# A block of attention and experts in one kernel: the shared network's weights prepared one stage earlier, and its down product issued two chunks behind

## The chip, the core and the metric

The kernel is one program on one core of a Trainium2 chip. The metric is device time in microseconds (us) of one execution, as the median of several runs. The engines are named as the profile names them: PE is TensorE, DVE is VectorE, ACT is ScalarE, POOL is GpSimd, SP is SyncE, which here only issues DMAs.

## What the reference computes

An input of 4 sequences of 2048 rows of 256 features goes through a modulated attention block and then through a modulated feed-forward block: eight routed experts, of which each row takes the two best, and one shared network that every row goes through. What matters here is the end of it:

```python
def _swiglu_mlp(x, wg, wu, wd):
    return jax.nn.silu(x @ wg) * (x @ wu) @ wd
...
y = jnp.einsum('te,etd->td', combine, expert_out).astype(x.dtype)
return y + _swiglu_mlp(identity, sw_gate, sw_up, sw_down)
...
x = x + gb * _L0_ffn_ref(h, ...)
```

The shared network has 704 hidden features (`sw_gate` and `sw_up` are 256 x 704, `sw_down` is 704 x 256). The modulated rows `h` are 8192 x 256.

## The kernel before, in words

The program runs stage after stage, with a barrier of all engines between two stages: setup, q/k/v, attention, a middle stage (projection, norm, routing), `expert_stage` and, last, `shared_stage`. Every stage has one instruction stream for each engine; the order within a stream is the order of the code, an engine does one thing after another, and semaphores order the engines among each other. Nothing is reordered.

All products of the last two stages run in two parts: a float32 value is split into a "high" part (a copy in float32r) and a "low" part (the value less its high part), and each product is the sum of high x high, low x high and high x low. ACT makes the high part of weights and rows, DVE or POOL the low part by a subtraction.

`expert_stage` goes over 39 blocks of 512 gathered rows. For a block it loads one expert's weights and the rows, splits them, and writes the outcome to DRAM (`made_dram`). In it POOL makes the low parts of two of the three weights.

`shared_stage` goes over 16 units `u` of 512 rows, in two buffers (`slot`). The 704 hidden features are `NC` = 6 chunks: five of 128 and, last, one of 64. In each unit:

- PE: `up(u, i)` (L2184 and on) makes gate and up products of chunk `i` into `ps_g` and `ps_u`, 12 matmuls of 512 columns (for the last chunk 6). It waits until the activation and the product two chunks back are done. `down(u, i)` (L2195 and on) multiplies the hidden chunk with `wd`, 12 matmuls of 256 columns, and waits for `hid_done` of that chunk. PE does `up(i)` and then `down(i - 1)`; after the first `up` of a unit comes the last `down` of the unit before.
- ACT: silu of each chunk (`act_g`, L2086; L2088 for the half chunk). Behind the third one (`i == 2`) it waits for the next unit's loads and makes `h_high` (`high_rows`, L2077).
- DVE: `hidden(u, i)` is three instructions: `hid_f` (L2129), the cast `hid_high` (L2133), the subtraction `hid_low` (L2135). Behind chunk 0 it does `finish` of the unit before, `total` (L2147) and `gated` (L2150); behind chunk 2 `h_low` of the next unit (`low_rows`, L2140); behind chunk 3 `mix_experts`, four `first` (L2114) and four `mix` (L2120), which weigh the rows of the two experts.
- POOL: eight gathers of expert rows for the next unit (`got`, L2051), and then `y_out` of this one (L2064), which waits for `gated`.
- SP: `load(u + 1)` (`h`, L2017, and `x`, L2019, 512 KB each), then the store of `y_out` of unit `u` (L2028). A load waits until the buffer is free: `h2_done` says that its rows have been split, and `out_done` that `y_out` of the unit two back, which reads the same `x` buffer, is made:

```python
            def load(u, slot):
                sp.wait_ge(h2_done, u + 1)
                sp.wait_ge(out_done, u + 1)
```

`out_done` starts at 2 and each `y_out` adds 1; `load(u + 1)` thus waits for `y_out(u - 1)`, and this for `finish(u - 1)`.

Before its first unit the stage loads its weights (L2008 to L2012), ACT copies them (L2096), DVE subtracts (L2174), and PE begins when all is split.

## Time and profile before

| | |
|---|---|
| time, median of 3 runs (lowest, highest) | 3312.66 us (3307.47, 3314.26) |
| the profiled execution: its own time, and its span | 3308.82 us, 3307.1 us |
| PE busy over the span | 2912.5 us, 88% |
| mean granted TensorE clock | 0.944 of full speed |
| last stage, from the barrier (2835.0) to the end of the span | 472.1 us |
| of that, PE's first matmul | 2853.12 |

A row of the timeline reads: start in us, duration in us, engine, line of the kernel, operation, output<-input, shapes, how many instructions are merged in the row, and in brackets how long the engine stood idle before it and on whom it waited. A matmul's duration is the time through the array; its pace is the distance between two starts. The profiled execution's own time is 1.7 us above its span.

### The profile page before, as it was taken

The numbers are of one execution on the slowest core, as the hardware profiler recorded it, in microseconds if no ns is written. First come the engines' busy times: TensorE is split into PE (matmuls) and PEld (weight loads), VectorE is DVE, ScalarE is ACT, GpSimd is POOL, SyncE is SP. The second block draws the span as 40 slices with busy tenths as digits, with TensorE's granted clock in tenths as the row PEclk, the third lists the DMA queues.
The fourth block names the chain that finished last, engine by engine and source line by source line (L and its number), as shares of the span: only waits on it lengthen the run. The fifth ranks groups of instructions, "written<-read, shape, count | busy, mean of one in ns | idle before, by whom it ended". The sixth has DMA issues, their size and how long they took to land. (4 is left out here: it accounts for less than half of the span.)

```text
span 3307.1 us, 61435 instructions
## 1 busy us (share of the span) xinstructions
PE 2912.5 (88%) x22508; PEld 1616.0 (49%) x22508; DVE 2518.0 (76%) x4678; ACT 1588.5 (48%) x2160; POOL 884.5 (27%) x1100
## 2 busy tenths in 40 slices
PE   6885699999999999999999996873999999788888
PEld 3553133333333333333333325763888888677776
DVE  5885989888898888898888914664777777566665
ACT  2542166666676666666666782221444444111111
POOL 5773010111110111101111112664222222333332
PEclk8997699999999999999999997775999999899999
DMA  4776111122111212111221005664444455332332
GB/s 132 204 209 186 49 35 47 48 54 53 43 44 49 54 48 57 38 46 48 55 52 43 20 8 160 212 198 167 155 155 155 156 159 156 105 94 85 96 97 73
DMA packets 388533, 317.93 MB, mean 96 GB/s; under 512 B 112720, under 2 KB 374844, under 8 KB 388288
## 3 DMA queue, kind: packets, MB, share of 16 engines
q1 hardware_dynamic: 370752, 277.67, 29.4%
q0 software_dynamic: 12288, 33.57, 3.0%
q10 hardware_dynamic: 5248, 3.41, 0.4%
q8 instruction: 155, 2.54, 0.3%
q14 instruction: 90, 0.74, 0.1%
HBM read 196.89 MB, written 116.93 MB: 95 GB/s over the span
## 5 line engine op out<-in xcount | busy, mean ns | idle before, releaser
L903 ACT ACTIVATE probs<-ps_s 128x1024 f32<-128x1024 f32 (+3 forms) x1280 | 1077.9, 896 | 599.2 <-PE ps_s L1071 598.6
L926 DVE TENSOR_REDUCE piece_rest<-ps_m 128x1 f32<-128x512 f32 (+2 forms) x1260 | 748.8, 646 | 91.8 <-PE ps_m L1046 42.0
L1071 PE MATMUL ps_s<-q_st,k_st 50*128 50x512 bf16 (+7 forms) x5120 | 594.4, 346 | 19.0 <-ACT probs L903 15.2
L1086 PE MATMUL ps_o<-probs,vs 128*32 128x512 f32 (+3 forms) x5120 | 600.8, 541 | 4.3 <-POOL probs L883 1.2
L883 POOL TENSOR_SCALAR_AFFINE_SELECT probs<-probs 128x256 f32<-128x256 f32 x512 | 204.9, 406 | 1481.2 <-ACT probs L903 1476.0
L926 DVE TENSOR_REDUCE piece_late<-ps_m 128x1 f32<-128x512 f32 x900 | 548.8, 666 | 33.0 <-PE ps_m L1038 17.9
L1038 PE MATMUL ps_m<-k_st,q_st 48*128 48x512 bf16 (+3 forms) x2400 | 407.5, 353 | 65.8 <-DVE piece_rest L926 48.1
L1038 PEld LDWEIGHTS ps_m<-k_st,q_st 48*128 48x128 bf16 x2400 | 106.9, 93 | 651.8 <-DVE piece_rest L926 339.0
L1071 PEld LDWEIGHTS ps_s<-q_st,k_st 50*128 50x128 bf16 (+1 forms) x5120 | 224.1, 95 | 250.8 <-ACT probs L903 91.0
L1803 ACT ACTIVATE act_g<-ps_g 128x512 f32<-128x512 f32 x117 | 69.9, 597 | 279.5 <-PE ps_u L1895 279.5
L1840 DVE TENSOR_TENSOR hid_f<-act_g,ps_u 128x512 f32<-128x512 f32 x117 | 80.5, 688 | 126.8 <-ACT act_g L1803 126.8
L1086 PEld LDWEIGHTS ps_o<-probs,vs 128*32 128x32 f32 x5120 | 101.2, 108 | 142.8 <-issue 96.9
L2086 ACT ACTIVATE act_g<-ps_g 128x512 f32<-128x512 f32 x80 | 47.5, 595 | 251.1 <-PE ps_u L2191 206.3
L1765 POOL TENSOR_TENSOR wu_low<-wu,wu_high 128x768 fp32r<-128x768 f32 x39 | 76.8, 1968 | 326.1 <-ACT wu_high L1791 326.1
L2202 PE MATMUL ps_d<-sd_high,hid_high 128*128 128x256 f32 x384 | 114.0, 297 | 47.5 <-DVE hid_low L2135 46.2
L1359 POOL DMA_INDIRECT expert_rows<-rows,at x128 | 133.3, 1041 | 66.9 <-issue 36.0
L1845 DVE TENSOR_TENSOR hid_low<-hid_f,hid_high 128x512 fp32r<-128x512 f32 x117 | 138.8, 1187 | 4.0
L2051 POOL DMA_INDIRECT got<-expert_made,at_now x128 | 128.7, 1006 | 49.1 <-issue 36.8
L1907 PE MATMUL ps_d<-wd_high,hid_high 128*128 128x256 f32 x468 | 136.0, 291 | 1.2 <-DVE hid_low L1845 1.2
L1907 PE MATMUL ps_d<-wd_low,hid_high 128*128 128x256 f32 x468 | 132.1, 282 | 0.0
L1907 PE MATMUL ps_d<-wd_high,hid_low 128*128 128x256 f32 x468 | 132.0, 282 | 0.0
L621 PE MATMUL ps_qk<-wqkv,h_t 128*128 128x512 f32 x256 | 122.8, 603 | 1.0 <-ACT h_t L559 1.0
(228 smaller groups left out, 5103.2 us busy)
## 6 DMA issues: line engine op xcount, KB each, us to landing
k_st<-qk_parts SPq DMA_DIRECT2D x768, 32.0 KB, 1.8
qk_parts<-parts SPq DMA_DIRECT2D x124, 192.0 KB, 2.9
q_st<-qk_parts SPq DMA_DIRECT2D x720, 32.0 KB, 1.8
x_r<-expert_rows SPq DMA_DIRECT2D x39, 512.0 KB, 4.6
expert_made<-made SPq DMA_DIRECT2D x39, 512.0 KB, 2.9
x_in<-in_L_attn_x_dram SPq DMA_DIRECT2D x32, 512.0 KB, 4.7
vs<-v_ones SPq DMA_DIRECT2D x64, 256.0 KB, 3.7
v_ones<-v_out SPq DMA_DIRECT2D x60, 256.0 KB, 4.7
```

The lines of the kernel that those rows point to most:

```text
L621: pe.matmul(ps_qk[:, t % 2, :], h_t[:, slot, c, t * P:(t + 1) * P], wqkv[:, c, 0:QK], start=(c == 0), stop=(c == DC - 1))
L883: pool.affine_select(out=block_now, in_=block_now, compare_op=ALU.is_ge, fill=0.0, base=0, pattern=[[0, 2], [1, P]], channel_multiplier=-1 ...
L903: act.activation(probs[:, u % PSLOTS, 2 * pair:2 * pair + 2, j * P:ST], ps_s[:, pair, :, j * P:ST], ACT.Exp, scale=SCALE).then_inc(exp_don ...
L926: v.tensor_reduce(dst, ps_m[:, bank, 0:n * w].rearrange("p (n w) -> p n w", n=n), AX.X, ALU.max) \
L1038: last[z] = pe.matmul(bank[:, i * w:(i + 1) * w], q_st[rows, slot, 0, a + i, qi * P:(qi + 1) * P], k_st[rows, slot, 0, a + i, kt * ST:kt * ...
L1071: last = pe.matmul(ps_s[:, pair, z, j * P:ST], k_st[rows, slot, half, pair, kc * P:(kc + 1) * P], q_st[rows, slot, half, pair, qt * ST + j ...
L1086: last = pe.matmul(ps_o[h * VW:(h + 1) * VW, j * P:ST], vs[:, slot, kc, h * VW:(h + 1) * VW], probs[:, u % PSLOTS, h, j * P:ST], start=(kc ...
L1359: pool.indirect_dma_start(rows_dram, bass.IndirectOffsetOnAxis(at[:, rslot, j:j + 1], 0), rows[:, rslot, j % TPS, :], None).then_inc(scatt ...
L1845: v.tensor_tensor(hid[1][:, i, :], hid_f[:, half, :], hid[0][:, i, :], ALU.subtract).then_inc(hid_done, 1)
L1907: last = pe.matmul(ps_d[:, t, :], hid[a][:, i, t * P:(t + 1) * P], wd_p[b][:, slot, i, :], start=(i == 0 and t % 2 == 0 and k == 0), stop= ...
L2051: pool.indirect_dma_start(got[:, slot, j, :], None, made_dram, bass.IndirectOffsetOnAxis(at_now[:, slot, j:j + 1], 0)) \
L2202: last = pe.matmul(ps_d[:, slot, t, :], hid[a][:, i % GS, t * P:(t + 1) * P], wd_p[b][:, i, :], start=(i == 0 and t % 2 == 0 and k == 0), ...
```

## The change

It has three parts.

1. The stage's weights and first rows are loaded in `expert_stage`. The buffers are now made ahead of both stages. SP issues six DMAs (five for weights, one for the rows of unit 0) behind the loads of the first two blocks. Behind its last block ACT makes the four high parts, DVE two low parts of the weights ahead of `take_made` and `h_low` of unit 0 behind it, and POOL the low part of `wd`. `shared_stage` begins with everything split.
2. `down` runs `LAG` = 2 chunks behind `up`: PE does `up(i)` and then `down(i - 2)`; the first two `up` of a unit are followed by the last two `down` of the unit before.
3. DVE's `finish` of the unit before and the copies of `weight_now` and `gb_now` stand behind chunk 2 instead of chunk 0, and `low_rows` behind chunk 4 instead of chunk 2. `mix_experts` stays behind chunk 3, and ACT's `high_rows` behind its third silu.

```diff
@@ expert_stage, SP, behind the first two blocks' loads
+            sp.wait_ge(padded, 4)
+            wg_s, wu_s, wd_s = W["wg"], W["wu"], W["wd"]
...
+            sp.dma_start(wg_s[:, :, 0:FS], sw_gate.rearrange("(c p) f -> p c f", p=P)).then_inc(next_in, 16)
+            sp.dma_start(wg_s[:, :, FS:SNC * P], up_cols[:, :, SFULL * P:FS]).then_inc(next_in, 16)
+            sp.dma_start(wu_s[:, :, :], up_cols[:, :, 0:SFULL * P]).then_inc(next_in, 16)
+            sp.dma_start(wd_s[:, 0:SFULL, :], sw_down[0:SFULL * P, :].rearrange("(j p) n -> p j n", p=P)).then_inc(next_in, 16)
+            sp.dma_start(wd_s[P - SHALF:P, SFULL, :], sw_down[SFULL * P:FS, :]).then_inc(next_in, 16)
+            sp.dma_start(W["h2"][:, 0, :, :].rearrange("p c t -> p (c t)"), h2_dram[0:P, :]).then_inc(next_in, 16)
@@ expert_stage, POOL, behind its last block
+            pool.wait_ge(next_high, 4)
+            pool.tensor_tensor(W["wd_p"][1][:, :, :], W["wd"][:, :, :], W["wd_p"][0][:, :, :], ALU.subtract)
@@ expert_stage, ACT, behind its last block
+            act.wait_ge(next_in, 16 * NEXT_DMAS)
+            for src, dst in ((W["wg"], W["wg_p"]), (W["wu"], W["wu_p"])):
+                act.activation(dst[0][:, :, :], src[:, :, :], ACT.Copy).then_inc(next_high, 1)
+            act.activation(W["h2_p"][0][:, 0, :, :], W["h2"][:, 0, :, :], ACT.Copy).then_inc(next_high, 1)
+            act.activation(W["wd_p"][0][:, :, :], W["wd"][:, :, :], ACT.Copy).then_inc(next_high, 1)
@@ expert_stage, DVE, behind its last block
+            for k, (src, dst) in enumerate(((W["wg"], W["wg_p"]), (W["wu"], W["wu_p"]))):
+                v.wait_ge(next_high, k + 1)
+                v.tensor_tensor(dst[1][:, :, :], src[:, :, :], dst[0][:, :, :], ALU.subtract)
             take_made(NB - 1, 0, NB // 2)
+            v.wait_ge(next_high, 3)
+            v.tensor_tensor(W["h2_p"][1][:, 0, :, :], W["h2"][:, 0, :, :], W["h2_p"][0][:, 0, :, :], ALU.subtract)
@@ shared_stage, ACT ahead of its first unit
-            act.wait_ge(w_in, 16 * W_DMAS)
-            act.wait_ge(padded, 1)
-            for src, dst in ((wg, wg_p), (wu, wu_p), (wd, wd_p)):
-                act.activation(dst[0][:, :, :], src[:, :, :], ACT.Copy).then_inc(w_high, 1)
-            high_rows(0, 0, 1)
+            act.sem_inc(h2_high, 1)
@@ shared_stage, DVE
                         hidden(u, i)
-                        if i == 0 and not (first and slot == 0):
+                        if i == LAG and not (first and slot == 0):
                             finish(u - 1, 1 - slot)
-                        if i == 0 and slot == 0:
+                        if i == LAG and slot == 0:
...
-                        if i == 2 and not (last and slot):
+                        if i == LAG + 2 and not (last and slot):
                             low_rows(u + 1, 1 - slot)
@@ shared_stage, PE
                         up(u, i, slot)
-                        if i > 0:
-                            down(u, i - 1, slot)
+                        if i >= LAG:
+                            down(u, i - LAG, slot)
                         elif not (first and slot == 0):
-                            down(u - 1, NC - 1, 1 - slot)
+                            down(u - 1, NC + i - LAG, 1 - slot)
```

The first place is DVE in the last unit but one, from its first chunk. Names: `act_g` is the silu, `hid_f`, `hid_high` and `hid_low` the hidden chunk and its parts, `total` and `gated` are `finish` of the unit before, `h_low` is `low_rows` of the unit behind. Before:

```order
L2129 TENSOR_TENSOR hid_f<-act_g,ps_u 128x512 [waits p5_hid,p5_silu]
L2133 CAST hid_high<-hid_f 128x512 [waits p5_down,p5_product]
L2135 TENSOR_TENSOR hid_low<-hid_f,hid_high 128x512 [waits p5_hid_high]
L2147 TENSOR_TENSOR total<-ps_d,mix 128x1024 [waits p5_gated,p5_got_used,p5_down]
L2150 TENSOR_TENSOR gated<-total,gb_now 128x1024 [waits p5_out,p5_summed]
L2163 COPY weight_now<-weight_all 128x16 [waits p5_got_used,p5_gated]
L2164 COPY gb_now<-gb 128x256
L2129 TENSOR_TENSOR hid_f<-act_g,ps_u 128x512 [waits p5_hid,p5_silu,p5_now]
L2133 CAST hid_high<-hid_f 128x512 [waits p5_down,p5_product]
L2135 TENSOR_TENSOR hid_low<-hid_f,hid_high 128x512 [waits p5_hid_high]
```

The same unit in the changed kernel, from its third chunk:

```order
L2150 TENSOR_TENSOR hid_f<-act_g,ps_u 128x512 [waits p5_hid,p5_silu]
L2154 CAST hid_high<-hid_f 128x512 [waits p5_down,p5_product]
L2156 TENSOR_TENSOR hid_low<-hid_f,hid_high 128x512 [waits p5_hid_high]
L2168 TENSOR_TENSOR total<-ps_d,mix 128x1024 [waits p5_gated,p5_got_used,p5_down]
L2171 TENSOR_TENSOR gated<-total,gb_now 128x1024 [waits p5_out,p5_summed]
L2184 COPY weight_now<-weight_all 128x16 [waits p5_got_used,p5_gated]
L2185 COPY gb_now<-gb 128x256
L2150 TENSOR_TENSOR hid_f<-act_g,ps_u 128x512 [waits p5_hid,p5_silu,p5_now]
L2154 CAST hid_high<-hid_f 128x512 [waits p5_down,p5_product]
L2156 TENSOR_TENSOR hid_low<-hid_f,hid_high 128x512 [waits p5_hid_high]
L2135 TENSOR_SCALAR first<-got,weight_now 128x256 [waits p5_gathered0]
```

`finish` has moved behind the third `hid_low`; the silu that the next `hid_f` waits for stands on ACT behind `high_rows`, in both kernels, and `h_low` has gone from ahead of `first` to behind the chunk after `mix`.

The second place is DVE at the end of `expert_stage`. Before, behind the last block's last cast:

```order
L1845 TENSOR_TENSOR hid_low<-hid_f,hid_high 128x512 [waits p4_hid_high]
L1850 COPY made<-ps_d 128x1024 [waits p4_stored0,p4_down]
L1656 UNCONDITIONAL_BRANCH
L2102 UNCONDITIONAL_BRANCH [waits barrier_Pool_Activation_PE_DVE_SP_release]
L2174 TENSOR_TENSOR sg_low<-sg_w,sg_high 128x1536 [waits p5_w_high]
L2174 TENSOR_TENSOR su_low<-su_w,su_high 128x1280 [waits p5_w_high]
L2174 TENSOR_TENSOR sd_low<-sd_w,sd_high 128x1536 [waits p5_w_high]
L2140 TENSOR_TENSOR h_low<-h_5,h_high 128x1024 [waits p5_h2_high]
```

And now:

```order
L1881 TENSOR_TENSOR hid_low<-hid_f,hid_high 128x512 [waits p4_hid_high]
L1907 TENSOR_TENSOR sg_low<-sg_w,sg_high 128x1536 [waits p4_next_high]
L1907 TENSOR_TENSOR su_low<-su_w,su_high 128x1280 [waits p4_next_high]
L1886 COPY made<-ps_d 128x1024 [waits p4_stored0,p4_down]
L1910 TENSOR_TENSOR h_low<-h_5,h_high 128x1024 [waits p4_next_high]
L1671 UNCONDITIONAL_BRANCH
L2123 UNCONDITIONAL_BRANCH [waits barrier_Pool_Activation_PE_DVE_SP_release]
L2150 TENSOR_TENSOR hid_f<-act_g,ps_u 128x512 [waits p5_hid,p5_silu]
```

Two subtractions stand ahead of the copy of the last block's outcome, one behind it, and the one of `wd` is POOL's.

## Rows read from the trace of the kernel before

**Rows 1.** The page's first part: busy time, share, instructions.
```profile
PE 2912.5 (88%) x22508; PEld 1616.0 (49%) x22508; DVE 2518.0 (76%) x4678; ACT 1588.5 (48%) x2160; POOL 884.5 (27%) x1100
```
**Rows 2.** Waits from 2866 to 3283: total us, times, longest.
```profile
ACT h_high L2077 <- DMA x<-x_mid: 81.8, 14, 7.2
...
PE ps_d L2202 <- DVE hid_low L2135: 45.0, 40, 3.2
```
**Rows 3.** Timeline of one unit, engines and the DMA queue, 3074 to 3101.
```profile
3074.72 0.40 PE L2191 MATMUL ps_g<-h_high,sg_high 128*128 128x512 f32 x1
...
3077.67 0.60 ACT L2086 ACTIVATE act_g<-ps_g 128x512 f32<-128x512 f32 x1 [5.42 <-PE ps_u L2191]
...
3080.09 1.22 DVE L2147 TENSOR_TENSOR total<-ps_d,mix 128x1024 f32<-128x1024 f32 x1
...
3081.34 1.22 DVE L2150 TENSOR_TENSOR gated<-total,gb_now 128x1024 f32<-128x1024 f32 x1
...
3082.71 2.52 POOL L2064 TENSOR_TENSOR y_out<-gated,x 128x1024 f32<-128x1024 f32 x1 [13.95 <-issue]
...
3085.26 0.38 SPq L2028 DMA_DIRECT2D out_dram<-y_out  x1
...
3085.99 0.60 ACT L2086 ACTIVATE act_g<-ps_g 128x512 f32<-128x512 f32 x1 [3.56 <-PE ps_u L2191]
...
3086.24 0.93 SPq L2019 DMA_DIRECT2D x<-x_mid  x1
...
3091.88 1.06 ACT L2077 ACTIVATE h_high<-h 128x1024 fp32r<-128x1024 f32 x1 [5.29 <-DMA x<-x_mid]
...
3092.84 0.58 ACT L2086 ACTIVATE act_g<-ps_g 128x512 f32<-128x512 f32 x1
...
3092.97 1.22 DVE L2140 TENSOR_TENSOR h_low<-h,h_high 128x1024 fp32r<-128x1024 f32 x1 [4.48 <-issue]
...
3095.97 1.20 DVE L2114 TENSOR_SCALAR first<-got,weight_now 128x256 f32<-128x256 f32 x4
...
3096.10 0.38 PE L2202 MATMUL ps_d<-sd_high,hid_high 128*128 128x256 f32 x1 [1.25 <-DVE hid_low L2135]
...
3098.79 0.68 DVE L2129 TENSOR_TENSOR hid_f<-act_g,ps_u 128x512 f32<-128x512 f32 x1
...
3099.96 0.69 DVE L2135 TENSOR_TENSOR hid_low<-hid_f,hid_high 128x512 fp32r<-128x512 f32 x1
```
**Rows 4.** Timeline of ACT: third silu of units 0, 1 and 15.
```profile
2865.39 0.60 ACT L2086 ACTIVATE act_g<-ps_g 128x512 f32<-128x512 f32 x1 [3.74 <-PE ps_u L2191]
...
2889.43 0.60 ACT L2086 ACTIVATE act_g<-ps_g 128x512 f32<-128x512 f32 x1 [3.56 <-PE ps_u L2191]
...
3282.91 0.60 ACT L2086 ACTIVATE act_g<-ps_g 128x512 f32<-128x512 f32 x1 [3.56 <-PE ps_u L2191]
```
**Rows 5.** Timeline of PE: where it resumes with its clock down.
```profile
2853.12 0.76 PE L2191 MATMUL ps_g<-h_high,sg_high 128*128 128x512 f32 x1 [22.73 <-DVE h_low L2140]
...
2858.10 0.40 PE L2191 MATMUL ps_g<-h_high,sg_high 128*128 128x512 f32 x1
...
3264.54 0.58 PE L2202 MATMUL ps_d<-sd_high,hid_high 128*128 128x256 f32 x1 [2.93 <-DVE hid_low L2135]
```
**Rows 6.** Timeline of several engines around the seam, 2814 to 2850.
```profile
2814.91 1.97 POOL L1769 TENSOR_TENSOR wd_low<-wd,wd_high 128x768 fp32r<-128x768 f32 x1 [1.40 <-ACT wd_high L1794]
...
2815.21 2.21 DVE L1845 TENSOR_TENSOR hid_low<-hid_f,hid_high 128x512 fp32r<-128x512 f32 x1
...
2826.13 0.60 ACT L1803 ACTIVATE act_g<-ps_g 128x512 f32<-128x512 f32 x1 [3.58 <-PE ps_u L1895]
...
2830.42 1.23 DVE L1850 COPY made<-ps_d 128x1024 f32<-128x1024 f32 x1 [1.79 <-PE ps_d L1907]
...
2835.00 0.39 SPq L2008 DMA_DIRECT2D sg_w<-in_L_ffn_sw_gate_dram  x1
...
2845.54 1.48 ACT L2096 ACTIVATE sg_high<-sg_w 128x1536 fp32r<-128x1536 f32 x1 [18.81 <-DMA sd_w<-in_L_ffn_sw_down_dram]
```

More of the change, by code:

```diff
@@ L54 @@
 E, F, FS = 8, 352, 704
+SNC = -(-FS // P)
+SFULL = FS // P
+SHALF = FS - SFULL * P
 EPS = 1e-5
@@ L156, in block_kernel, with late @@
                      steps_dram, plan_dram)
-        expert_stage(nc, C, rows_dram, made_dram, w_gate, w_up, w_down)
-        shared_stage(nc, C, h2_dram, x1_dram, made_dram, sw_gate, sw_up, sw_down, out_flat)
+        with ExitStack() as last:
+            def late(name, shape, dt=F32):
+                return last.enter_context(nc.sbuf_tensor(name, shape, dt))
+            W = dict(
+                wg=late("sg_w", [P, DC, SNC * P]), wu=late("su_w", [P, DC, SFULL * P]), wd=late("sd_w", [P, SNC, D]),
+                wg_p=[late(f"sg_{part}", [P, DC, SNC * P], F32R) for part in PARTS],
+                wu_p=[late(f"su_{part}", [P, DC, SFULL * P], F32R) for part in PARTS],
+                wd_p=[late(f"sd_{part}", [P, SNC, D], F32R) for part in PARTS],
+                h2=late("h2_5", [P, 2, DC, ST]),
+                h2_p=[late(f"h2_{part}", [P, 2, DC, ST], F32R) for part in PARTS],
+            )
+            expert_stage(nc, C, W, rows_dram, made_dram, w_gate, w_up, w_down, h2_dram, sw_gate, sw_up, sw_down)
+            shared_stage(nc, C, W, h2_dram, x1_dram, made_dram, out_flat)
 def stand_alone(eng, held):
@@ L1691, in expert_stage @@
         padded = sem("p4_padded")
+        next_in = sem("p4_next_in")
+        next_high = sem("p4_next_high")
+        NEXT_DMAS = 6
         w_high = sem("p4_w_high")
@@ L1758, in _ @@
             pool.wait_ge(padded, 3)
+            pool.memset(W["wd"][0:P - SHALF, SFULL, :], 0.0).then_inc(padded, 1)
+            pool.wait_ge(padded, 4)
             pool.sem_inc(wu_done, 1)
@@ L1940, in shared_stage @@
     GS = 3
+    LAG = 2
     PICKS = TOPK * TPS
@@ L1952, in shared_stage @@
         gb, weight, made_at = C["gb"], C["weight"], C["made_at"]
-        wg = sb("sg_w", [P, DC, NC * P])
-        wu = sb("su_w", [P, DC, full * P])
-        wd = sb("sd_w", [P, NC, D])
-        wg_p = [sb(f"sg_{part}", [P, DC, NC * P], F32R) for part in PARTS]
-        wu_p = [sb(f"su_{part}", [P, DC, full * P], F32R) for part in PARTS]
-        wd_p = [sb(f"sd_{part}", [P, NC, D], F32R) for part in PARTS]
-        h2_p = [sb(f"h2_{part}", [P, 2, DC, ST], F32R) for part in PARTS]
-        h2 = sb("h2_5", [P, 2, DC, ST])
+        wg_p, wu_p, wd_p, h2, h2_p = (W[k] for k in ("wg_p", "wu_p", "wd_p", "h2", "h2_p"))
         x1 = sb("x1_5", [P, 2, TPS, D])
@@ L2007, in _ @@
         def _(sp):
-            sp.dma_start(wg[:, :, 0:FS], sw_gate.rearrange("(c p) f -> p c f", p=P)).then_inc(w_in, 16)
-            sp.dma_start(wg[:, :, FS:NC * P], sw_up.rearrange("(c p) f -> p c f", p=P)[:, :, full * P:FS]).then_inc(w_in, 16)
-            sp.dma_start(wu[:, :, :], sw_up.rearrange("(c p) f -> p c f", p=P)[:, :, 0:full * P]).then_inc(w_in, 16)
-            sp.dma_start(wd[:, 0:full, :], sw_down[0:full * P, :].rearrange("(j p) n -> p j n", p=P)).then_inc(w_in, 16)
-            sp.dma_start(wd[UPPER, full, :], sw_down[full * P:FS, :]).then_inc(w_in, 16)
             def load(u, slot):
@@ L2016, in load @@
                 sp.wait_ge(out_done, u + 1)
-                sp.dma_start(h2[:, slot, :, :].rearrange("p c t -> p (c t)"), h2_dram[ds(u * P, P), :]) \
-                    .then_inc(in_done[slot], 16)
+                if u:
+                    sp.dma_start(h2[:, slot, :, :].rearrange("p c t -> p (c t)"), h2_dram[ds(u * P, P), :]) \
+                        .then_inc(in_done[slot], 16)
+                else:
+                    sp.sem_inc(in_done[slot], 16)
                 sp.dma_start(x1[:, slot, :, :], x1_dram[ds(u * ST, ST), :].rearrange("(t p) d -> p t d", p=P)) \
@@ L2038, in _ @@
         def _(pool):
-            pool.memset(wd[0:P - HALF_CHUNK, full, :], 0.0).then_inc(padded, 1)
-            pool.wait_ge(padded, 1)
             pool.sem_inc(out_done, 2)
@@ L2170, in body @@
                             mix_experts(u, slot, it)
-            for k, (src, dst) in enumerate(((wg, wg_p), (wu, wu_p), (wd, wd_p))):
-                v.wait_ge(w_high, k + 1)
-                v.tensor_tensor(dst[1][:, :, :], src[:, :, :], dst[0][:, :, :], ALU.subtract).then_inc(w_done, 1)
-            low_rows(0, 0)
             body(0, True, False)
@@ L2221, in _ @@
                 body(it, False)
-            down(NST - 1, NC - 1, 1)
+            for i in range(NC - LAG, NC):
+                down(NST - 1, i, 1)
 _INS = ['L0_attn_x', 'L0_attn_w_qkv', 'L0_attn_w_proj', 'L0_attn_b_proj', 'L0_ffn_gate_w', 'L0_ffn_w_gate',
```

13 lines of the change are left out of this document (4 added, 9 removed).

## The prediction, made before the changed kernel ran

> **What bounds the kernel now.** I read the page's first part, the waits of the last stage, and then one unit of it as a timeline; the other stages keep their instructions, apart from six DMA issues and a memset. PE is busy for 88% of the span [rows 1], but in the last stage two kinds of wait stand out [rows 2]: PE waits 45.0 us, 40 times, for `hid_low` ahead of `down`, and ACT waits 81.8 us, 14 times, for the next unit's loads ahead of `h_high`. The first is what a `down` two chunks behind takes away. The second is the one to look at. ACT takes things in order, so its fourth silu stands behind `h_high`, and `h_high` behind a load that is issued only after `y_out` of the unit before. The reader should see this as one chain in the timeline [rows 3]: first silu 3077.67, `total` 3080.09, `gated`, `y_out` 3082.71, store issue 3085.26, load issue 3086.24, `h_high` 3091.88, fourth silu 3092.84. It takes 15.17 us. It starts at the unit's first silu, while PE goes on in chunks of 4.16 us (3085.99 less 3077.67, halved); by its end PE has waited only 1.25 us (3096.10). A unit lasts (3282.91 - 2889.43) / 14 = 28.11 us from third silu to third silu [rows 4].
>
> **The unit after the change.** `finish` now stands behind `hidden(2)`, two chunks later. The load still waits for `y_out` of the unit before, and ACT's `high_rows` still stands ahead of the fourth silu. So the same 15.17 us now start at the third silu, where the fourth is due 4.16 us later. I go round the loop once from the third silu, all from [rows 3]:
>
> - third silu to `total` 2.42, to `y_out` 2.62, to the store's issue 2.55, to `h_high` 6.62, to the fourth silu 0.96: together 15.17.
> - Late loads: over 14 units ACT's wait for them has a mean of 81.8 / 14 = 5.84 us [rows 2] against 5.29 in this unit: +0.55. They had some cover before, now none.
> - fourth silu to the end of `hidden(3)` 2.42 (as the first silu to `total`), `first` and `mix` 2.82 (3095.97 to 3098.79), `hidden(4)` 1.86 (3098.79 to 3100.65).
> - `h_low` of the next unit 1.22; it now stands here, and PE waits for it ahead of the next unit's `up(0)`.
> - PE from `up(0)` to the third silu: 3085.99 - 3074.72 = 11.27. This part holds three `up` and two `down`, as before.
>
> The sum is 35.3 us, against 28.11. Is PE really out of work? Behind the third silu it has `down(0)`, `up(3)`, `down(1)`, `up(4)`, `down(2)`, which end 9.5 us after it: 2 x 4.16 and a `down` of 1.4, less 0.2. (`up(0)` takes 2.95 us from its start at 3074.72 to the silu; with 0.2 of that for the hand-over, a choice of mine, an `up` is 2.75 and a `down` the other 1.4 of 4.16.) `up(5)` needs the fourth silu and its product, at 15.7 + 1.3 = 17.0: a wait of 7.5 us (1.3 is the silu's 0.6 and `hid_f`'s 0.7). Behind it stand `down(3)` and the next unit, until `h_low` at 24.0. DVE idles in the same hole, since `hidden(3)` needs that silu; POOL's gathers run there and are needed only a unit later. The loop is taken by the loads of units 2 to 15, 14 times: 14 x (35.3 - 28.11) = +100.7 us. The 40 short waits for `hid_low` are gone, but they lie inside the 28.11 that the new period replaces, so nothing more is gained for them.
>
> **The clock.** After a stall of 2.93 us PE resumed at half pace (its `down` at 3264.54 is a matmul of 0.58 us where 0.38 is usual), while the wait of 1.25 left it at full pace [rows 3, 5]. The longest of the 40 waits is 3.2 us [rows 2], so such a fall is rare before. A hole of 7.5 us will set it to 1.2 GHz in each unit. `up(5)` and `down(3)` at half pace still end at 17.0 + 2 x 2.8 = 22.6, before `h_low`. What counts is whether the clock is back at `up(0)`, 7 us after the resumption, with a second hole of some 2 us between. An `up(0)` at half pace takes 4.98 us (2858.10 - 2853.12) instead of 2.75 [rows 5]: 2.2 more. The bounds are 0 and, if `down` behind it is slow too, 3.6 a unit. I take half an `up`, 1.1, for 14 units: +15. The Trainium skill says in "TensorE: Matmul & The Clock Gate" (HAM oscillation) that where a loop waits for a DMA in every tile, the gate closes in every tile and the penalty is paid each time. The stall of 2.93 us agrees; by that rule each unit pays in full, and that is the first rival below.
>
> **The seam.** Before, PE began the stage at 2853.12 [rows 5], 18.1 us behind the barrier, for loading and splitting [rows 6]. Now ACT copies behind its last silu (2826.73): 1.48 for 1536 columns [rows 6], so by size 5.2 for all four, to 2832.0. POOL's subtraction of 1536 columns is twice its 768 of 1.97: to 2835.9. DVE does two subtractions (by size from `h_low`, 1.8 and 1.5) from 2828.6 (2826.13 and 2.42, as from silu to `total`), then `made`, to 2833.2 where it ended at 2831.65; the barrier came 3.35 us after that end, so 2836.6. `h_low` falls beside POOL: a subtraction of 0.69 [rows 3] took 2.21 beside POOL's [rows 6], so I let it wait until 2835.9, to 2837.1. With half a microsecond for the barrier PE begins at 2837.6: -15.5. If the copy `made` were held by POOL too, the barrier would come 3 us later. The Trainium skill ("SBUF — State Buffer", two separate sides) says that the port pair that both engines share is locked against an operation with two SBUF inputs. `made` reads PSUM and would pass; by that rule the seam stays at 2837.6. The trace shows no `made` beside POOL.
>
> From there to unit 1's third silu it was 36.3 us; now `up(0)` at half pace 4.98, two more `up` without a `down` 5.5, 0.2 to the silu, and a full-pace unit 23.6: 34.3, I take 34.6, so -1.7. The loads of this stretch are issued at once and hide.
>
> **What costs nothing.** The six DMA issues of SP (0.4 to 0.9 us each by [rows 3], so 2 to 6 us) stand behind both blocks' loads and ahead of a store that is due a block later. If the cover were gone, PE's second block would lose up to 6 us; I take 0. The tail: the last `down` no longer waits for its chunk, -0.5.
>
> **Sum.** Span 3307.1 - 15.5 - 1.7 - 0.5 + 100.7 + 15 = 3405; own time 1.7 above it: 3407. The profiled execution before took 3308.82, the median was 3312.66, 3.8 more. Forecast: **3411 us**, 3.0% slower.
>
> **Rivals.**
>
> - *The clock stays low at the start of every unit*, through `up(0)` and the `down` behind it: 3.6 instead of 1.1 a unit, +35: 3446. For it: the second hole, and the rule above. Against: at 2853.12 the clock was back after 5 us of work [rows 5]. 14%.
> - *Faster: the loads land before the fourth silu needs them*, and the lag does what it can. Place: store issue to `h_high`. Then PE never waits and a unit lasts 5 x 4.16 + 2.8 = 23.6: 3411 - 15 - 14 x 11.7 = 3232. It decides where the loop has lost (100.7 + 15 - 17.7) / 14 = 7.0 us: below that price the kernel is faster. From the store's issue to `h_high` it would have to be 0.2 us instead of 7.2 (6.62 and 0.55), so only if the load did not wait for `y_out` at all. The code and the order of issues in [rows 3] (store, then loads, 0.03 us behind `y_out`) speak against it. 4%.
> - *The chain is read rightly but does not bind*: something that I left out, such as a shorter way from `finish` to the load, gives back most of the 7.2 us a unit and leaves about the time of before: 3312. 2%.
> - The forecast with the clock's term between 0 and 2 a unit, and the seam 3 us either way: 3392 to 3430. 80%.
>
> **How the numbers follow.** The forecast and the clock rival hold 94%. The range of the likeliest is 3392 to 3430; I take 3385 to 3440 for 8 in 10, with the lower end for loads that always land as in [rows 3] (-8) and a hole that does no harm. What a measurement of this kernel can tell from no change is about 0.2%, 6.6 us. Faster 5%, the same 2%, slower 93%.
>
> **What would show it.** ACT: the fourth silu of units 1 to 14 starts about 15.7 us after the third, with `h_high` waiting some 12 to 14 us for the load. PE: one wait of 7 to 8 us ahead of the last `up` of a unit, on a silu or its product, and one of 1.5 to 3 ahead of the next unit's first, on `h_low`; no more on `hid_low`. Third silu to third silu 35 to 37 us. Granted clock in the last stage near 0.85. PE's first matmul of the stage at 2837 to 2841. The prediction is wrong if the period is under 30 us, or if the fourth silu doesn't stand behind `h_high`.

## The result: 3.5% slower, and the profile after

| | before | after |
|---|---|---|
| time, median (lowest to highest) | 3312.72 us (3307.47 to 3314.26), 4 runs | 3429.70 us (3422.96 to 3433.95), 4 runs |
| ratio to before, 95% interval | | 1.0354 [1.0334, 1.0374] |
| profiled execution, own time and span | 3308.82, 3307.1 us | 3433.95, 3432.2 us |
| mean granted TensorE clock | 0.944 | 0.927 |
| a unit of the last stage | 28.11 us | 37.46 us |

The forecast was 3411 us, with 3385 to 3440 around it. The first part of the page after has the same number of matmuls as before [rows 1], but 44 us more of PE's busy time, and a smaller share:

```profile
PE 2956.3 (86%) x22508; PEld 1658.9 (48%) x22508; DVE 2494.7 (73%) x4677; ACT 1587.0 (46%) x2160; POOL 878.5 (26%) x1101
```

The waits of the last stage after, from 2866 to the end of the span (engine, instruction, whom it waited for: total us, times, longest single one), which answer to [rows 2]:

```profile
ACT h_high L2102 <- DMA x<-x_mid: 204.6, 14, 15.1
...
PE ps_g L2208 <- DVE hid_f L2150: 88.0, 11, 8.4
...
PE ps_g L2208 <- DVE h_low L2161: 30.2, 15, 2.3
PE ps_g L2208 <- ACT act_g L2111: 23.4, 3, 7.9
...
PE ps_d L2219 <- DVE hid_low L2156: 0.8, 2, 0.5
```

The wait that the distance of two chunks was to take away is gone: 45.0 us before `down`, now 0.8. In its place stand 14 waits of about 8 us (88.0 and 23.4 together), and 15 of 2 us for `h_low`. Above them ACT's wait for the load has grown from 81.8 us to 204.6.

One unit as a timeline, ACT, DVE, POOL, PE and the DMA queue in order of time, answers to [rows 3]:

```profile
3107.53 0.60 ACT L2111 ACTIVATE act_g<-ps_g 128x512 f32<-128x512 f32 x1 [3.56 <-PE ps_u L2208]
...
3109.95 1.22 DVE L2168 TENSOR_TENSOR total<-ps_d,mix 128x1024 f32<-128x1024 f32 x1
...
3112.57 2.39 POOL L2089 TENSOR_TENSOR y_out<-gated,x 128x1024 f32<-128x1024 f32 x1 [24.68 <-issue]
...
3114.99 0.38 SPq L2055 DMA_DIRECT2D out_dram<-y_out  x1
...
3115.48 0.44 SPq L2042 DMA_DIRECT2D h<-h_t  x1
...
3123.00 1.06 ACT L2102 ACTIVATE h_high<-h 128x1024 fp32r<-128x1024 f32 x1 [14.87 <-DMA x<-x_mid]
...
3123.96 1.06 ACT L2111 ACTIVATE act_g<-ps_g 128x512 f32<-128x512 f32 x2
...
3125.41 0.77 PE L2208 MATMUL ps_g<-h_high,sg_high 128*128 128x512 f32 x1 [8.18 <-DVE hid_f L2150]
...
3131.08 1.22 DVE L2161 TENSOR_TENSOR h_low<-h,h_high 128x1024 fp32r<-128x1024 f32 x1
...
3132.36 0.66 PE L2208 MATMUL ps_g<-h_high,sg_high 128*128 128x512 f32 x1 [2.22 <-DVE h_low L2161]
...
3136.99 0.60 ACT L2111 ACTIVATE act_g<-ps_g 128x512 f32<-128x512 f32 x1 [8.06 <-PE ps_u L2208]
...
3145.31 0.60 ACT L2111 ACTIVATE act_g<-ps_g 128x512 f32<-128x512 f32 x1 [3.56 <-PE ps_u L2208]
```

The loop can be read off row by row. The third silu (3107.53) lets `total` go, then `y_out`, the store, the load, and `h_high` 15.47 us later. The fourth and fifth silu, merged in one row, stand right behind it, though the fourth's products had been there for long (`up(3)`'s last matmul started at 3111.27). PE's last `up` waits 8.18 us, DVE works off its queue until `h_low`, and the next unit's first `up` starts at 3132.36. From third silu to third silu that is 37.78 us; over 14 units it is 37.46, from two rows of ACT's timeline that answer to [rows 4]:

```profile
2882.79 0.60 ACT L2111 ACTIVATE act_g<-ps_g 128x512 f32<-128x512 f32 x1 [3.56 <-PE ps_u L2208]
...
3407.27 0.60 ACT L2111 ACTIVATE act_g<-ps_g 128x512 f32<-128x512 f32 x1 [3.56 <-PE ps_u L2208]
```

The seam, where the expert stage ends, answers to [rows 6]. The rows are of ACT, DVE and POOL, and PE's first matmul of the last stage:

```profile
2830.55 0.60 ACT L1834 ACTIVATE act_g<-ps_g 128x512 f32<-128x512 f32 x1 [3.58 <-PE ps_u L1936]
2831.05 1.48 ACT L1849 ACTIVATE sg_high<-sg_w 128x1536 fp32r<-128x1536 f32 x1
...
2834.53 1.47 ACT L1851 ACTIVATE sd_high<-sd_w 128x1536 fp32r<-128x1536 f32 x1
...
2836.05 1.22 DVE L1886 COPY made<-ps_d 128x1024 f32<-128x1024 f32 x1
...
2836.08 3.42 POOL L1806 TENSOR_TENSOR sd_low<-sd_w,sd_high 128x1536 fp32r<-128x1536 f32 x1 [14.78 <-ACT sd_high L1851]
...
2837.18 3.40 DVE L1910 TENSOR_TENSOR h_low<-h,h_high 128x1024 fp32r<-128x1024 f32 x1
...
2841.19 0.77 PE L2208 MATMUL ps_g<-h_high,sg_high 128*128 128x512 f32 x1 [6.37 <-DVEq L2127]
```

From the last silu to PE's first matmul it was 26.99 us [rows 5, 6]; it is now 10.64. That is the gain of the change, 16.35 us. The last silu itself came 4.42 us later in this execution than in the one before: 4.05 of that had gathered in the stages ahead of `expert_stage`, whose work nobody touched, and 0.37, at most the price of the six added DMAs, between the start of `expert_stage` and that silu.

**Where the time went**, by spans: 4.05 (earlier stages) + 0.37 - 16.35 (seam) + 5.29 (unit 0 and the start of unit 1: 41.60 us from PE's first matmul to unit 1's third silu, against 36.31) + 14 x (37.46 - 28.11) = 130.9 + 0.74 (the end) = 125.0; measured 3432.2 - 3307.1 = 125.1.

### The profile page after: what moved, and what is told of

The parts are those of the page before. It is cut to its first block and busy times, and to the rows that moved or that the text cites. A ratio compares the mean times of both kernels' runs of the same rounds, so it can differ in the third digit from the quotient of the medians.

```text
span 3432.2 us, 61434 instructions
## 1 busy us (share of the span) xinstructions
PE 2956.3 (86%) x22508; PEld 1658.9 (48%) x22508; DVE 2494.7 (73%) x4677; ACT 1587.0 (46%) x2160; POOL 878.5 (26%) x1101
## 3 DMA queue, kind: packets, MB, share of 16 engines
q8 instruction: 155, 2.54, 0.3%
## 5 line engine op out<-in xcount | busy, mean ns | idle before, releaser
L1086 PE MATMUL ps_s<-q_st,k_st 50*128 50x512 bf16 (+7 forms) x5120 | 595.2, 346 | 19.0 <-ACT probs L918 15.2
L941 DVE TENSOR_REDUCE piece_late<-ps_m 128x1 f32<-128x512 f32 x900 | 549.1, 667 | 33.9 <-PE ps_m L1053 17.3
L2150 DVE TENSOR_TENSOR hid_f<-act_g,ps_u 128x512 f32<-128x512 f32 x80 | 54.8, 685 | 299.3 <-ACT act_g L2111 160.5
L2208 PE MATMUL ps_g<-h_high,sg_high 128*128 128x512 f32 x192 | 90.8, 473 | 147.9 <-DVE hid_f L2150 88.0
L1876 DVE TENSOR_TENSOR hid_f<-act_g,ps_u 128x512 f32<-128x512 f32 x117 | 80.5, 688 | 127.3 <-ACT act_g L1834 127.3
L2089 POOL TENSOR_TENSOR y_out<-gated,x 128x1024 f32<-128x1024 f32 x16 | 39.1, 2445 | 374.9 <-issue 338.5
```

The costliest lines, as they stand in the source:

```text
L941: v.tensor_reduce(dst, ps_m[:, bank, 0:n * w].rearrange("p (n w) -> p n w", n=n), AX.X, ALU.max) \
L1086: last = pe.matmul(ps_s[:, pair, z, j * P:ST], k_st[rows, slot, half, pair, kc * P:(kc + 1) * P], q_st[rows, slot, half, pair, qt * ST + j ...
L1876: v.tensor_tensor(hid_f[:, half, :], act_g[:, half, :], ps_u[:, half, :], ALU.mult).then_inc(product, 1)
L2208: last = pe.matmul(dst[:, i % 2, :], w[a][:, c, i * P:(i + 1) * P], h2_p[b][:, slot, c, :], start=(k == 0), stop=(k == DC * len(PRODUCTS) ...
```

## Experiments

The theory was the *load chain*: the load of the next unit's rows hangs on `finish`, and ACT's fourth silu on that load. Its rivals: *the distance itself* (a `down` two chunks behind makes the loop long, wherever `finish` stands), and *the work moved into the seam*. Below, `DOWN` is the distance of `down`, `FIN` the chunk behind which `finish` stands, `LOW` that of `low_rows`. The kernel after is 2, 2, 4 and the kernel before 1, 0, 2. Each ratio is to runs of the kernel before on the same chip.

**1. The seam alone.**

```diff
-    LAG = 2
+    DOWN, FIN, LOW = 1, 0, 2
```

> The changed kernel with the order of the last stage put back: down one chunk behind, finish and the copies behind chunk 0, low_rows behind chunk 2. Only the work moved into expert_stage is left of the change. Theory L (the lag moved finish, and with it the load and ACT's fourth silu, two chunks later): the units are those of before, 28.1 us from third silu to third silu, and the seam gives its 16 us: 3313 - 16 - 2 = 3295 us, up to 3301 if the 6 us that unit 0 lost come with the seam. Theory W (the loss comes with the weights' new place, by their addresses or by DMAs in another stage): still above 3400 us.

3300.23 us (3297.59 to 3304.67, 9 runs), ratio 0.9969 [0.9959, 0.9979]. The seam is not what made the kernel slow; it is worth 0.3%. From last silu to first matmul it took 10.63 us, as in the kernel after, so the seam gains 16.4 us here too. But the spans differ by 9.7 only: from PE's first matmul to unit 1's third silu it took 43.33 us against 36.31, and ACT's third and fourth silu of unit 0 are late with no engine named (the profile's word is `remote`). More on this in 9.

```profile
2849.25 0.60 ACT L2111 ACTIVATE act_g<-ps_g 128x512 f32<-128x512 f32 x1 [6.31 <-remote]
...
2858.50 0.60 ACT L2111 ACTIVATE act_g<-ps_g 128x512 f32<-128x512 f32 x1 [7.71 <-remote]
```

**2. The distance alone**, in the kernel before: `down` two chunks behind, with `finish` and `low_rows` where the change has them, and no work moved across the seam.

```diff
-                        if i == 0 and not (first and slot == 0):
+                        if i == LAG and not (first and slot == 0):
                             finish(u - 1, 1 - slot)
```

> The kernel before with the lag alone: down two chunks behind, finish and the copies behind chunk 2, low_rows behind chunk 4; weights loaded and split in the last stage as before. Theory L: a unit lasts 37.5 us as in the changed kernel, and the seam costs its 16 us again: 3430 + 16 = 3446 us, or 3440 without unit 0's 6 us. Theory W: near 3313 us.

3438.65 us (3437.50 to 3444.08, 4 runs), ratio 1.0392 [1.0374, 1.0409]; 37.45 us a unit (from `h_high` of unit 2 to that of unit 15, by 13). The whole loss is this part.

**3. `finish` back to chunk 1, and to chunk 0**, `down` still two behind; one run each.

```diff
-    LAG = 2
+    DOWN, FIN, LOW = 2, 1, 4
```

> The changed kernel with finish and the copies behind chunk 1 instead of chunk 2; the lag of down stays at two chunks. Theory L: y_out, the load, h_high and the fourth silu all come 4.2 us sooner, a unit lasts 33.3 us, 14 x 4.2 = 58 us less: 3371 us. Theory D (two chunks of lag are slow in themselves, by PE waiting for silu or by its clock): no change, 3430 us.

> The same with finish and the copies behind chunk 0, where DVE has to wait for the last down of the unit before, which PE now does behind up(1). Theory L: total starts some 5.7 us after the first silu instead of 10.7 (third silu 8.3 and 2.4), so a unit is 5 us shorter than in the changed kernel, 32.4 us: 3360 us, and less if PE's hole gets too short for the clock to fall. Theory D: 3430 us.

3356.96 us and 3354.34 us (single runs, no interval), 32.55 and 32.08 us a unit. The distance is the same and the loss is more than halved, so most of the loss isn't the distance itself. One chunk earlier gives back 4.9 us a unit, 0.7 more than a chunk of 4.16, and the time was 14 us below what I expected. The trace shows where 0.5 of the 0.7 is: in 5 of 14 units TensorE's clock was up at the next unit's first `up`, and over all 14 that took 4.17 us to its silu on average, where the kernel after needs 4.65 (see 6). The second chunk gives only 0.5. Why so little is a row of the waits of the second kernel:

```profile
DVE total L2168 <- PE ps_d L2219: 49.0, 16, 3.4
```

`finish` at chunk 0 waits there for the last `down` of the unit before, which PE makes only behind `up(1)`: 49.0 us in 16 waits, 3.06 on average. So the distance has a price on this chain after all. The prediction has nothing of it; the expectation of this run had.

**4. The load freed from the chain.** `h` is loaded a unit earlier on a semaphore of its own, as soon as its buffer is free, and ACT waits for `h` alone; `x` still waits for `y_out`. With the distance 2 (`DOWN, FIN, LOW = 2, 2, 2`), and with 1 (`1, 0, 2`).

```diff
+            def load_h(u, slot):
                 sp.wait_ge(h2_done, u + 1)
-                sp.wait_ge(out_done, u + 1)
...
+                    if not last:
+                        load_h(u + 2, slot)
                     if not (last and slot):
-                        load(u + 1, 1 - slot)
+                        load_x(u + 1, 1 - slot)
...
-                act.wait_ge(in_done[slot], turn_no * 32)
+                act.wait_ge(h_in[slot], turn_no * 16)
```

> The changed kernel with the load split: the rows h of unit u + 2 are issued as soon as unit u has split its own (one unit ahead), on their own semaphore, and only x waits for y_out; ACT's high_rows waits for h alone; low_rows is back behind chunk 2, behind finish. down stays two chunks behind. Theory L (what costs is that ACT's fourth silu stands behind a load that waits for y_out): no hole in PE, a unit at PE's own pace of 23.6 to 24.3 us, 14 x (28.1 - 23.9) = 59 us below the kernel before and 16 more for the seam: 3238 us. Theory D (the lag is slow in itself): above 3400 us.

> The same split of the load with down one chunk behind and finish behind chunk 0, as before. Theory L: ACT's wait is gone here too; what stays are short waits of PE for hid_low, above all behind first and mix (0.4 to 1 us a unit): 24.6 us a unit, 3250 us. So the lag, on this ground, is worth some 10 us. If the lag is worth nothing, both are the same; if the waits for hid_low stay at 1.5 us twice a unit, 3275 us.

3254.81 us (3250.09 to 3255.36, 5 runs), ratio 0.9816 [0.9803, 0.9829], and 3254.02 us (3252.99 to 3260.93, 5 runs), ratio 0.9818 [0.9805, 0.9831]; 24.77 and 24.70 us a unit. With the load off the chain the kernel after turns from 3.5% slower to 1.8% faster, and `h_high` waits for no DMA. The first version also puts `low_rows` back behind chunk 2, which was not tried alone; in the kernel after PE's waits for `h_low` add up to 30.2 us and the clock behind them costs 1.7 us a unit, together about 4 of the 12.7 us by which the unit got shorter, so the most of it is the load. The first came 17 us above what I expected, and the distance, with the places of `finish` and `low_rows` that go with it, was worth nothing. Both keep a wait of PE, of the version with distance 2 in the whole last stage and then of that with 1 from 2866 to 3230:

```profile
PE ps_g L2212 <- DVE hid_f L2154: 12.9, 13, 1.4
```

```profile
PE ps_d L2223 <- DVE hid_low L2160: 10.4, 25, 2.3
```

The last number of such a row is the longest single wait: on average they are 1.0 and 0.4 us. The expectations below take it for the length of each.

**5. The next unit's rows split first**: `h_high` behind the first silu, `h_low` at chunk 0 or 1, where DVE has time, so that the later hidden values come sooner.

```diff
-                        if i == 2 and not (last and slot):
+                        if i == 0 and not (last and slot):
                             high_rows(u + 1, 1 - slot, it + (1 + slot))
```

> The version with the early load of h and the down product two chunks behind (e5_early_h, 3254.81 us, period 24.80 us), with the next unit's first rows ahead of the hidden values: h_high behind the first silu and h_low at chunk 0. In e5_early_h the PE waited 13 times 1.4 us for hid_f in the last stage. Load-chain theory: h is there more than a unit ahead, so nothing waits for a DMA; if the rows ahead of the last hidden values are what the PE waits for, the period falls by about 1.1 us to 23.7 us and the time to about 3239 us. Rival (the hidden values of the first chunks are then delayed instead by the h_low now ahead of them, 1.2 us): no change, 3252 to 3258 us.

> The same with the down product one chunk behind (e6_early_h_lag1, 3254.02 us, period 24.70 us, PE waits for hid_low 26 times 2.3 us in it): finish at 0, h_high behind the first silu, h_low at chunk 1. If the second chunk of distance is worth anything once h comes early, this one stays above e7_rows_first, at 3245 to 3250 us, since each wait for hid_low costs the PE what the distance would cover; if the distance is worth nothing, both give the same, about 3240 us.

With distance 2 (`2, 2, 0`) 3231.81 us (3228.90 to 3234.09, 5 runs), ratio 0.9760 [0.9747, 0.9773], 23.60 us a unit. With distance 1 (`1, 0, 1`) 3252.95 us (3247.61 to 3254.87, 5 runs), ratio 0.9821 [0.9808, 0.9835], 24.80 us a unit. Now the second chunk of distance is worth 21 us, again with `finish` and `low_rows` at the places that go with it. From 2866 to 3170 in the first of them PE has no gap (window, its length, then busy us and instructions of PE, weight loads, DVE, ACT and POOL; clock; DMA share; GB/s):

```profile
2866.00:3170.00 304.00, 304.00 (x1782) 269.30 (x1781) 245.09 (x388) 58.40 (x91) 132.33 (x124) 1.00 0.35 109
```

23.60 is what the prediction worked out for a unit that never waits (5 x 4.16 + 2.8). This version is the fastest of all: 79 us below the kernel before on its chip. It came 7 us below what I expected, the other 3 above; part of the 7 may lie in unit 0, where PE had no gap this time (28.00 us busy from 2842 to 2870), though a silu of ACT was late there too.

**6. The loads ahead of the store**, in the kernel after.

```diff
-                    if not (last and slot):
-                        load(u + 1, 1 - slot)
+                    if not u:
+                        load(1, 1)
                     sp.wait_ge(out_done, u + 1 + 2)
+                    if u + 2 < NST:
+                        load(u + 2, slot)
                     sp.dma_start(out_flat[ds(u * ST, ST), :].rearrange("(t p) d -> p t d", p=P), y_out[:, :, :]) \
```

> The changed kernel with the loads of h and x of the unit after next issued on SP ahead of the store of y_out, behind the same wait for y_out. Queue theory: the landing of h, 8.0 us from the store's issue to h_high, holds 0.5 us of issue and some 1.2 to 1.5 us of the store's own 512 KB that go ahead of the load; the loop is then 1.7 to 2.0 us a unit shorter, 14 times, less nothing else: 3402 to 3406 us. If the store's transfer shares the engines with the loads wherever it stands, only the issue is saved, 7 us: about 3423 us. If neither counts, 3430 us.

3393.41 us (3389.81 to 3395.32, 4 runs), ratio 1.0248 [1.0232, 1.0264]; 36 us below the kernel after, more than the queue theory gave. The store ahead of the loads did cost about what it said: over 14 units `h_high` now comes 6.14 us after the first issue on average, not 7.69, and ACT's waits for the load add up to 183.8 us instead of 204.6, 1.5 us less a unit (1.7 to 2.0 were expected). But a unit is 34.70 us, 2.8 less. The rest is the clock. A *hole* here is a stretch in which PE has no work; the kernel after has two in each unit, one ahead of the last `up` and one ahead of the next unit's first. These are matmuls of PE in one unit of this version: the last `up`, the end of the `down` behind it, and the start of the next unit's first `up`.

```profile
3138.29 0.77 PE L2210 MATMUL ps_g<-h_high,sg_high 128*128 128x512 f32 x1 [6.40 <-issue]
3138.85 0.63 PE L2210 MATMUL ps_g<-h_low,sg_high 128*128 128x512 f32 x1
3139.28 0.63 PE L2210 MATMUL ps_g<-h_high,sg_low 128*128 128x512 f32 x1
...
3143.34 0.41 PE L2221 MATMUL ps_d<-sd_high,hid_low 128*128 128x256 f32 x1
3145.07 0.51 PE L2210 MATMUL ps_g<-h_high,sg_high 128*128 128x512 f32 x1 [1.31 <-DVE h_low L2163]
3145.41 0.39 PE L2210 MATMUL ps_g<-h_low,sg_high 128*128 128x512 f32 x1
3145.64 0.40 PE L2210 MATMUL ps_g<-h_high,sg_low 128*128 128x512 f32 x1
```

After 6.40 us without work PE resumes at 1.2 GHz (starts 0.43 us apart). After the second, shorter hole of 1.31 it resumes at 2.4 GHz (0.23 apart) and stays there: `up(0)` to its silu takes 3.05 us. So it was in 12 of 14 units, with second holes of 1.31 to 1.73 us. In two, behind 1.79 and 1.93, the clock fell during `up(0)`, which took 4.61 and 4.64; these units lasted 36.2 and 36.4 us, the others 34.2 to 34.6. In the kernel after, this hole was 1.73 to 2.31 us and `up(0)` took 4.63 to 4.66 in 14 of 14 units. The hole's length is not the only thing that differs: behind the first hole the clock was back after 3.5 to 4.6 us in the kernel after, here in no unit before 4.58 and in 9 of 14 not until the second hole. Where it comes back earlier, `down(3)` ends earlier and the second hole is longer, so these runs don't tell the two apart.

**7. `h_high` behind the fourth silu**, in the kernel after.

```diff
-                        if i == 2 and not (last and slot):
+                        if i == 3 and not (last and slot):
                             high_rows(u + 1, 1 - slot, it + (1 + slot))
```

> The changed kernel with ACT's h_high of the next unit behind the fourth silu (chunk 3) and not ahead of it, everything else as it is. Load-chain theory: the fourth silu, and with it the last hidden values, no longer wait for the load; the loop loses what stands between h_high and the last up products but still waits for h_low and h_high ahead of up(0) of the next unit, so it gets shorter by about 4.9 us a unit, some 69 us: about 3361 us, more if the clock still falls in each unit. Rival D (the down product's distance of two chunks is itself what makes the loop long): 3430 us as before.

3363.29 us (3361.99 to 3367.60, 4 runs), ratio 1.0161 [1.0146, 1.0177]; 32.70 us a unit, 4.8 less than after, where 4.9 was expected. So the order of ACT's two instructions is the other half of the loop. With no distance changed and no load moved, more than half of the loss goes.

**8. PE's holes filled** with matmuls of 128x256 that nobody reads, in the kernel after: 60 ahead of the last `up` of a unit and 30 ahead of the first of the next.

```diff
+                    if u > 1:
+                        fill(slot, 30)
                     pe.wait_ge(h2_done, u + 3)
...
+                        if u and i == NC - 1 and u < NST - 1:
+                            pe.wait_ge(summed, u + 2)
+                            fill(1 - slot, 60)
                         up(u, i, slot)
```

> The changed kernel with matmuls whose result nobody reads, in the PE's own holes: 60 of 128x256 ahead of the last up product of each unit and 30 ahead of the first of the next, at 0.117 us each 7.0 of the 8.2 us and 3.5 of the about 4 us that the PE stands still there. The loop of load, silu and product is untouched. Clock theory: the PE then enters the last up product and the first of the next unit at 2.4 GHz; up(0) to its silu takes 2.95 us again and not 4.63, which is 1.7 us a unit, 14 times, 24 us: about 3406 us. If the clock is not what made up(0) slow, or if it lies beside the loop, 3430 us; if the added matmuls delay the real ones, above 3430 us.

3413.83 us (3410.81 to 3417.05, 4 runs), ratio 1.0310 [1.0293, 1.0327]. PE's stretches in one unit: the filling, the next unit's first matmul, and the silu that it leads to.

```profile
3118.78 3.76 PE L2226 MATMUL ps_d<-sd_high,sg_high 128*128 128x256 f32 x30
3122.72 0.50 PE L2208 MATMUL ps_g<-h_high,sg_high 128*128 128x512 f32 x1 [0.19 <-DVE h_low L2161]
3123.06 0.39 PE L2208 MATMUL ps_g<-h_low,sg_high 128*128 128x512 f32 x1
```

```profile
3125.79 0.60 ACT L2111 ACTIVATE act_g<-ps_g 128x512 f32<-128x512 f32 x1 [7.10 <-PE ps_u L2208]
```

From `up(0)` to its silu it now takes 3.07 us instead of 4.63: the clock was what made it slow, and 1.6 us a unit its price. The kernel gained 16 us, not 24: `h_high` came 15.63 us behind the third silu on average (14.84 to 17.64), not 15.22, so that a unit is 36.27 us, 1.2 less. Why the load took 0.4 longer there, the runs don't show. More work for PE, less time: it would be no remedy, since it treats what the loop leaves behind.

**9. Unit 0.** In the kernel after, its fourth silu is late as well, and no engine is named:

```profile
2853.08 0.60 ACT L2111 ACTIVATE act_g<-ps_g 128x512 f32<-128x512 f32 x1 [3.36 <-PE ps_u L2208]
...
2863.11 0.60 ACT L2111 ACTIVATE act_g<-ps_g 128x512 f32<-128x512 f32 x1 [8.49 <-remote]
```

Of the 8.49 us ACT stood 7.1 with its products there (`up(3)`'s last matmul started at 2855.58 and took 0.39). The trace has three loads and 16 gathers in this stretch, eight for unit 0 and eight for unit 1. The experiment holds the second eight back:

```diff
                 pool.wait_ge(got_used, u + 1)
+                if u == 1:
+                    pool.wait_ge(silu_done, 2 + 5)
```

> The changed kernel with the eight gathers of unit 1 held in POOL's queue until the fifth silu of unit 0; nothing else moves. In the changed kernel's trace the fourth silu of unit 0 came 5.9 us late (2863.11 where the spacing before it, 4.16 us after 2853.08, puts it at 2857.24), with waits that name no engine of this kernel, while 98 us-rate gathers (98 to 115 GB/s) and copies of x ran. If the gathers beside it are the cause, unit 0 loses these 5.9 us and the time is about 3424 us; if the delay belongs to the entry of the stage whatever moves beside it, the fourth or fifth silu of unit 0 is late by 5 to 6 us again and the time is 3430 us (up to 3432 us if unit 1 then waits for the gathers).

```profile
2847.41 0.60 ACT L2113 ACTIVATE act_g<-ps_g 128x512 f32<-128x512 f32 x1 [2.12 <-PE ps_u L2210]
...
2851.57 0.60 ACT L2113 ACTIVATE act_g<-ps_g 128x512 f32<-128x512 f32 x1 [2.61 <-PE ps_u L2210]
```

The fourth silu comes 4.16 us after the third, on time, and from PE's first matmul (2837.38) to unit 1's third silu (2871.26) it takes 33.88 us instead of 41.60. The prediction had 34.6. So the silu is late because those eight gathers run there, right behind the first eight. Gathers alone don't do it: the held ones ran from 2857.75 on, and the silus beside them kept their 4.16 us. From PE's first matmul to the end of the span it took 583.0 us against 591.0, so the gain of 7.7 is kept. In the medians it is small: 3423.23 us (3420.42 to 3425.43, 4 runs), ratio 1.0340 [1.0323, 1.0357], whose interval overlaps that of the kernel after. What ACT waits for there (`remote`) the trace doesn't say.

## Why the prediction was right, and where its sizes were off

- **The chain round the unit: right.** It was read from the trace of before, and each link is there after: third silu to `total` 2.42 (2.42), to `y_out` 2.62 (2.62), to the store's issue 2.42 (2.55), to the fourth silu through `h_high` 8.97 (8.13 with the 0.55 for late loads). Experiments 3, 4 and 7 break it at three places, and each time more than half of the loss goes: 3357 us where the chain gave 3371, 3255 where it gave 3238, 3363 where it gave 3361. Its signs came as listed, most a little above their size: the fourth silu 16.2 us after the third (15.7), a wait of 14.6 for the load (12 to 14), holes of 7.5 to 8.4 and 1.7 to 2.3, a unit of 37.46 (35 to 37), a granted clock of 0.86 from 2883 to 3407 (0.85).
- **The late loads: mis-sized.** I took 14.76 us from third silu to `h_high`; the mean is 15.2 (204.6 / 14 of waiting, and 0.6 of silu): +0.45 a unit. What makes the 0.45 is open. Experiment 6 shows only a part of the whole: with the store's 512 KB ahead of the loads on the same queue `h_high` comes 1.5 us later than without.
- **The clock: right that it falls in each unit, mis-sized.** `up(0)` to its silu took 4.63 us instead of 2.95 [rows 3], 1.68 a unit where I took 1.1. The rival with 3.6 is refuted, for the clock was back before `down` behind it. I had taken the fall ahead of the last `up` and asked whether the clock would still be low at `up(0)`. It was back by then, 3.5 to 4.6 us after PE resumed, and fell a second time, at `up(0)` itself, behind the hole of 2 us. I had sized it from stalls of 1.25 and 2.93 us [rows 3, 5], and this one lay between. I had also read only one row of the four longest waits of the kernel before (2.93 to 3.19 us): behind two of them PE resumed at full pace and fell 1.4 us later, as at 3013.29 (rows in the last section). The Trainium skill ("TensorE: Matmul & The Clock Gate", HAM oscillation) says that a loop with a DMA wait in each tile pays in each tile. The trace of after agrees, 14 times in 14; experiment 6 waits for a DMA in each unit too; its clock was low at the last `up` in 14 of 14, where it held nothing up, and at `up(0)` in 2 of 14.
- These two make 1.03 of the 1.06 us by which a unit is longer than 35.3 + 1.1, together 14.8 us.
- **The seam: right.** -16.35 against -15.5. `made` began on DVE with POOL at its subtraction beside it and took 1.22, as long as alone [rows 6], while `h_low` took 3.40 instead of 1.22 until POOL was done. That is the Trainium skill's rule that I had weighed ("SBUF — State Buffer", two separate sides), and this trace agrees in both halves: `made` has its source in PSUM, `h_low` two in SBUF.
- **Unit 0: wrong, by 7 us once.** "The loads of this stretch are issued at once and hide" failed. They do hide from their own consumers; but ACT's silu was late beside the gathers, +5.3 instead of -1.7. Without them the size was right (33.9 against 34.6). The profiled execution came 27 us above its forecast of 3407 us: 15.2 for the units (the 14.8, and 0.4 by which +15 is short of 14 x 1.1), 7.0 here, 4.05 in the stages ahead, 1.6 for the six DMAs and the end, less 0.9 at the seam. The median stood 4.3 us below that execution where I had put it 3.8 above the profiled one, which leaves the 18.7 us between 3411 and 3429.70. So 8 of the 27 us were made up by chance in the choice of execution, and the median lies at the very edge of the 3392 to 3430 that I had called likeliest.
- **Nothing for the six DMAs** (0.37), and -0.5 for the end (+0.74): small enough.
- **The faster rival** was said to need a load that does not wait for `y_out` at all, and then 23.6 us a unit and 3232 us. Experiment 5 is that version, with 23.60 us a unit, and took 3231.81 us; the agreement to 0.2 us is in part luck, for the 3232 hold 3.8 us by which the median was to lie above the profiled execution, and here it lay 0.8 above. Freeing the load was not enough, though (3254.81): it took the order of the splits on ACT and DVE as well. For the change as it was made the rival is refuted.

## What to carry to other kernels

Before moving an instruction later in its queue, follow what hangs on it all the way round the loop: a step that gives PE two chunks of slack was also the step that freed the next load, and an in-order queue with a load's consumer ahead of urgent work (the fourth silu behind `h_high`) turns a late load into a stall of everything. An idea that loses can be right on its own: the same distance of two chunks cost 3.9% with the load on the chain, was worth nothing with the load off it, and gained 0.6% once the order of the splits let it work. Where a stall is inevitable, it can cost more than its own time, because TensorE's clock falls with it (here 1.7 us a unit at `up(0)`).
